# Row numbers of a chunk in a four-layer graph network: one register load of 28 from an aligned row in place of two of 14

## What is computed

```
x = layernorm(x + gcn_gcn(x))      # layer 0: two graph convolutions, 128 -> 512 -> 128
x = layernorm(x + gat(x))          # layer 1: attention over the edges of a node, 4 heads
x = layernorm(x + weighted_gat(x)) # layer 2: 8 heads, edge weights
x = layernorm(x + gat_ffn(x))      # layer 3: 4 heads, then a feed-forward part
# one graph convolution, with the self loops added to the edges:
out[d] = sum over edges (s -> d) of  xw[s] * dinv[s] * dinv[d]
```

## Time and profile before

| | us |
|---|---|
| runs | 5918.64, 5927.08, 5931.12 |
| profiled execution | 5925.47 |
| its span (first to last instruction) | 5923.7 |
| of it build (from the first take to the end of the last) | 217 to 799 |
| of it reading | 855 to 1123 |
| DVE busy over the span | 3247.8 (55%) |
| PE busy over the span | 3257.2 (55%) |
| PE / DVE busy, 303 to 394 us | 77.6 / 86.4 of 91 |
| PE / DVE busy, 950 to 1020 us | 68.2 / 27.0 of 70 |

### The profile page before, as it was taken

One profiled execution on the slowest core, in us unless ns is written; L12 is line 12 of the kernel. 1 busy time (PEld: TensorE's weight loads), 2 busy tenths in 40 slices (PEclk: granted clock), 3 DMA queues, 4 the chain that ended last, 5 costly groups with the idle time before them and its releaser, 6 DMA issues. The chain is left out here.

```text
span 5923.7 us, 64720 instructions
## 1 busy us (share of the span) xinstructions
PE 3257.2 (55%) x16208; PEld 1977.8 (33%) x16208; DVE 3247.8 (55%) x10115; ACT 2411.6 (41%) x5229; POOL 2310.7 (39%) x2409
## 2 busy tenths in 40 slices
PE   2887887514555555562255555555523555565563
PEld 1333353303333333341133333333311334333342
DVE  6998953504544545585155555555822455454576
ACT  1766620114434444443244443444433444443453
POOL 3000002173455454415445445444064545545422
PEclk7999998756777777786577777777756777777786
DMA  2111124221122111101111111111021111112110
GB/s 74 59 59 78 59 84 166 85 62 34 46 47 48 44 46 44 45 22 44 38 47 47 45 47 46 46 46 43 4 53 37 46 45 47 46 45 47 46 25 23
DMA packets 127649, 298.66 MB, mean 50 GB/s; under 512 B 45413, under 2 KB 74973, under 8 KB 123713
## 3 DMA queue, kind: packets, MB, share of 16 engines
q0 software_dynamic: 74976, 155.58, 11.4%
q1 hardware_dynamic: 52320, 139.24, 7.1%
HBM read 241.28 MB, written 53.38 MB: 50 GB/s over the span
## 5 line engine op out<-in xcount | busy, mean ns | idle before, releaser
L1399 POOL DMA_INDIRECT work<-table,lane_src x2184 | 2071.5, 948 | 1992.4 <-PE psum L1553 1100.5
L1496 PE MATMUL psum<-work 128*128 128x396 bf16 (+1 forms) x5850 | 1445.0, 395 | 844.1 <-issue 624.5
L1438 ACT ACTIVATE work<-work,middle_node_number 128x384 f16<-128x384 f16 x1587 | 958.1, 604 | 2003.8 <-DMA work<-table,lane_src 711.7
L1714 DVE TENSOR_TENSOR node_sums<-node_sums,psum 128x136 f32 x2418 | 592.6, 294 | 1444.1 <-remote 854.9
L1553 PE MATMUL psum<-work 128*128 128x136 f32 x4836 | 830.6, 337 | 847.6 <-DVE node_sums L1714 659.9
L1496 PEld LDWEIGHTS psum<-work 128*128 128x128 bf16 x5850 | 649.4, 113 | 1475.2 <-issue 997.0
L1553 PEld LDWEIGHTS psum<-work 128*128 128x128 f32 x4836 | 773.3, 239 | 959.1 <-issue 795.3
L1441 ACT ACTIVATE work<-work 128x384 bf16<-128x384 f16 x1587 | 829.4, 523 | 51.8
L715 PE MATMUL psum<-work 128*128 128x448 f16 x2100 | 460.0, 357 | 48.1 <-DVE node_sums L709 44.9
L744 DVE TENSOR_SCALAR work<-work 128x400 f16<-128x400 f16 x1568 | 462.5, 315 | 0.0
L772 PE MATMUL psum<-work 128*128 128x400 f16 x1568 | 340.3, 341 | 112.0 <-DVE work L744 90.2
(11 more groups left out here) (360 smaller groups left out, 2573.5 us busy)
## 6 DMA issues: line engine op xcount, KB each, us to landing
counts<-work SPq DMA_DIRECT2D x14, 2800.0 KB, 8.2
work<-counts SPq DMA_DIRECT2D x14, 2800.0 KB
work<-table,lane_src POOLq DMA_INDIRECT x2184
work<-spread SPq DMA_DIRECT2D x78, 256.0 KB
work<-masks SPq DMA_DIRECT2D x78, 128.0 KB
work<-source_rows SPq DMA_DIRECT2D x39, 192.0 KB
spread<-node_sums SPq DMA_DIRECT2D x4, 896.0 KB
table<-work SPq DMA_DIRECT2D x10, 330.0 KB
```

Source lines behind the costliest of these rows:

```text
L1399: pool.indirect_dma_start(m.ring[:, s % SLOTS, 0:F + H], None, m.d_table[H], bass.IndirectOffsetOnAxis(ap=m.src[:, s:s + 1], axis=0)).then ...
L1438: act.activation(away, rows_of(g, u), ACT.Abs, bias=m.low_tile[:, hi:hi + 1]).then_inc(far_known, 1)
L1496: mm = pe.matmul(aid_banks[:, k, 0:3 * (F + H)], hot_of(g, u)[:, k * P:(k + 1) * P], m.all_thirds[:, :, hi, 0:F + H], start=(hi == 0), sto ...
L1714: dve.tensor_tensor(to, to, sum_slot(s), ALU.add).then_inc(summed, 1)
```

## The change

`CREGS` becomes 28, the length of a chunk: `take_sum` loads at k = 0 only, 28 registers by one instruction. `count_row` is followed by two unused floats, so that `cj_row`, and all that lies behind it up to `low_last`, begins 8 bytes later.

```
-CREGS = 14
+CREGS = CHUNK = 28
...
-CHUNK = 28
...
     m.count_row = m.arena[:, late:late + EDGE_TILES]
-    late += EDGE_TILES
+    late += -(-EDGE_TILES // 4) * 4
     m.cj_row = m.arena[0:1, late:late + CG * P].bitcast(I32)
...
-    late = 4 * 8 * LANES + 17 * P + EDGE_TILES + CG * P + CCOLS // 2
+    late = 4 * 8 * LANES + 17 * P + -(-EDGE_TILES // 4) * 4 + CG * P + CCOLS // 2
     m.low_last = m.arena[:, late:late + CG * P]
```

## The result

The changed kernel takes 5888.64 us (median of 4 runs, 5879.82 to 5894.95), the kernel before 5928.01 us beside it (4 runs): ratio 0.9935, with an interval of 0.9918 to 0.9952, or 39.4 us less. The forecast was 5886. The profiled execution took 5894.95 us, with a span of 5893.2. Every line number from 70 on is one lower than before (L703 is the register load, L708 the add, L742 and L743 the one-hots).

A forecast was written before the change was run, and what follows sets the result against it. DVE was taken to set the build's pace, with register-load gaps on the path. Savings of 15.9 (build), 12 (reading to chunk 5) and 13.0 (rest) made 40.9 us: 5884.6, by the median 5886; range 5860 to 5906.

The forecast's parts named there:

- Load of 28: Register load of a chunk: seven aligned groups of four at 0.299 us, 2.09 us in all.
- C: Rival: registers come one by one, a load takes 6.35 us; 54 us slower, 5981; chance 0.07.
- D: Rival: no change, the load only fills time DVE's sequencer owes anyway, so the gaps stay; chance 0.06.
- eight plain gaps: Build, DVE gaps before a chunk's first add, not at a loop top: 10.1 us falling to about 1.0, 9.1 saved.
- Build: Build of the counts: 9.1 from plain gaps, 4.4 at loop tops, 2.4 from the last take; 15.9 us saved.
- The extra at the loop tops: Build, load behind the branch takes 4.5 us more, taken as something the load waits for; 4.4 us saved.
- rival A: Small gain: loop-top stall runs beside the load and the crawl costs the same; 29.5 us saved, some 5898; chance 0.19.
- Reading to chunk 5: First part of the reading: earlier takes and a shifted crawl let PE start chunk 5 sooner; 12 us saved.
- the crawl: Reading: DVE's sequencer needs 700 ns for almost every instruction; tied to POOL's 35 indirect DMAs, expected from 908.9 to 949.6.
- B: Rival: the crawl goes, 40 us from the reading's first part; 69 us saved, 5858; chance 0.10.
- Rest of the reading: Reading behind chunk 5: PE's waits before chunks 11 to 13 and the last take shrink; 13.0 us saved.
- Nothing else moves: Everything outside build and reading, including phases from 1124 us with the same code: 0 us.

The follow-up runs named there:

- e3: Changed kernel with the reading's chunks cut into register loads of 1 to 28 registers at various start addresses; 4361.31 us (one run).
- e1: Kernel before with one load of 28 registers but without the padding, so the row stays 8 bytes behind a multiple of 16; 4493.66 us, ratio 1.0231.
- e5: Changed kernel with SyncE storing each build chunk eight units later and its loop written out; 4335.87 us, ratio 0.9873 to the kernel before.
- e4: Changed kernel with VectorE's build loop unrolled (last ten chunks written out, no branch); 4321.13 us, ratio 0.9837 to the kernel before.
- e9: Changed kernel with POOL's 35 indirect DMAs of the reading in five bursts of seven; 5925.76 us, ratio 0.9866 to the kernel before.
- e8: Changed kernel with POOL's 35 indirect DMAs of the reading held back until take 4 is done; 5878.38 us (one run).
- series 3: Follow-up runs on one chip: the padding alone, and POOL's indirect DMAs held back; the kernel before took 5931.86 us there.
- series 1 and 2: Follow-up runs on one chip where neither kernel crawls; the kernel before took 4391.94 and 4390.85 us there.
- series 4: Follow-up runs with POOL's indirect DMAs in bursts of seven; the kernel before took 6007.31 us there.

## Why the prediction was right

**Load of 28.** 2.09 us forecast, 1.853 measured. The mechanism was right (aligned fours), the size 0.24 us too long, for the reason that e3 shows; the 75 ns a register that were called a floor held the fixed 0.10 us too, and the load costs 66. C, registers one by one (5981), fell with it: it is what happens without the padding (e1). D fell with the eight plain gaps.

**Build, 15.9 forecast, 18.2 measured.** The plain gaps gave all of their 10 us, not 9.1, since the shorter load fits wholly under the sequencer's lead. The tops fell from 7.4 to 5.8 us a piece and not to 6.3, which is 6.6 us instead of 4.4; but 2.2 us of that came back as the gap behind the branch, 8.3 us in four, where before DVE stood 6.1 us there for PE. The last take gave 2.7 for 2.4 (from the end of PE's last product to the last add, 11.1 us before and 8.4 after). These make 17.4 of the 18.2; the rest has no row.

**The extra at the loop tops.** It was taken as something that the load waits for. It is the store of the finished chunk that reads SBUF just then, as e5 shows: same branch, store 15 us later, load 1.853 us. The slowing is a factor, not an addend: a load that lies wholly inside the store takes about 3.2 times as long (1.10 to 3.5, 1.32 to 4.3, 1.85 to 6.0). The load of 7.68 us (3.18 alone) before outlasted its store by 1.0 us; inside the store it spent 6.7 us on what takes 2.2 alone, three times as long. So a load shortened by 1.3 us shortened the gap by more than that. The stall behind a taken branch that the Trainium skill tells of (Runtime: NRT & Kernel Launch, Instruction fetch mechanics) fits the 2.05 us before the first one-hot, which are gone without the branch (e4); that they are instruction fetch is not shown. They are not what makes the load long, and rival A's first reason fell.

**Reading to chunk 5, 12 forecast, 6.8 measured: the step that failed.** Held: POOL's first DMA moved with take 1 (3.8 us sooner from the start of the reading, 3.9 forecast), and the crawl moved with it. What failed is the path from there to chunk 5, in three places. First, the crawl began 6.4 us after POOL's first DMA and not 7.7, so that 18 adds of take 2 fell into it and not 12: take 2 ended 10 us sooner (86.5 us after PE's first matmul, not 96.7), not 15, and PE's wait became 28 us and not 24. Second, chunk 4 took 19.5 us, where 14.35 were reckoned: I had the crawl act on DVE's instructions only, and left out PE's clock after its wait. Third, the signal for take 3 came only with the end of the crawl (933.1), so that all of take 3, its load too, lay behind it: 8.0 us where 5.9 were reckoned. Chunk 5 started when chunk 4 was done, 106.2 us after PE's first matmul, forecast 100.5, before 112.9. Of the 5.7 us between, 3.1 are the later end of take 3 (103.6), the other 2.6 are chunk 4's. With or without a crawl (6.8 and 6.4 us) nearly the same is gained, so the 33 us that it costs (268.9 - 235.4 before, 248.1 - 214.8 after) are a toll that this change neither pays nor saves. Rival A had this right (it put 5 on this part), B was wrong: to lose the crawl its cause has to be spread (e9, as far as its chip would crawl), not met at another time (e8).

**Rest of the reading, 13.0 forecast, 14.0 measured,** by its steps: PE's 6.73 us wait and the 1.6 us behind it gone, the rest in the waits before chunks 12 and 13 and in the last take.

**Nothing else moves.** The hidden layer took 0.6 us more and the attention 7.7 in one pair of traces, 0.8 in the other. The sum was 40.9; the traces give 38.1 to the end of the reading and the medians 39.4. One term 5 us too high met others 3.3 too low, so that the forecast of 5886 lies 3 us from the median is in part luck: with this term as measured and the others as forecast, the sum would have been 36.

**Open.** What in POOL's DMAs slows the sequencers, why on some chips and not on others, and whether the "issue" of the attention there is the same thing: the runs show both together and no more. Not tried: a store made slower, so that it would spread its reads.

## What to carry to other kernels

Lay rows that registers are loaded from at multiples of 16 bytes and load them in multiples of four; then keep each load shorter than the sequencer's lead (2.2 us here), and look which DMA reads SBUF while it runs. Where a run of instructions takes several times its usual spacing on more than one engine at once, look for a burst of GpSimd's indirect DMAs beside it, and spread it before tuning anything that stands in its shadow. A gain in a stretch with such a toll in it should be worked out without the toll first: here the traces without it show 6.4 us and those with it 6.8, while the working through the crawl gave 12.

## What the runs showed of the hardware that I had not expected

- A register load runs three times as slowly while a DMA reads a large tile out of SBUF (7 us at 410 GB/s): 1.85 us become 6.0. Two more cases in the kernel before are the load at 776.2 us (4.352 us), in the store of the last chunk, and the one at 1085.6 us (3.966), in the stores at the end of the reading. The chunk loads of the reading, which write to SBUF, slow none: before, the load at 1079.0 us, beside one of them, took 3.191 us.
- 28 registers take 1.85 us from an aligned address, 6.25 us from one 8 bytes further, 11.06 us if a store lies inside it.
- A taken branch at the end of a loop turn costs VectorE 2.05 us and its sequencer's lead of 2.2 us, and with that the cover of the next load; without the four of them the build was 33 us shorter, the store's part included (e4).
- On the chips of the first measurement and of series 3, 35 indirect DMAs in a row bring DVE and PE to one add and one matmul per 2.8 us (0.21 and 0.19 are normal), from 6 to 10 us after the start of the first until 6 us after that of the last, and a signal came 37 us late. On the chip of series 1 and 2 they don't, and neither do bursts of seven in series 4.
